# VectorE instead of GpSimd subtracts the row maximum from the first chunk of every attention block

## What is computed

```python
def _gat_layer(x, W, adj):
    proj = x @ W
    Wh, Ws = jnp.split(proj, 2, axis=-1)
    scores = Wh @ Ws.T
    a = jax.nn.softmax(scores, axis=-1) * adj
    out = a @ Wh
    out = out + x
    return jax.nn.leaky_relu(out, NEG_SLOPE)
```

## Time and profile before

| | |
|---|---|
| median of 3 runs | 1641.16 us (1640.25 to 1642.18) |
| the profiled execution, its own time | 1643.23 us |
| its span, first to last instruction | 1641.4 us |
| attention, first scores to end | about 518 to 1641 us of the span |
| PE busy | 1568.4 us, 96% of the span |
| DVE busy | 1183.7 us, 72% |
| ACT busy | 1086.6 us, 66% |
| POOL busy | 996.9 us, 61% |
| mean granted TensorE clock | 0.995 of full speed |

### The profile page before, as it was taken

One profiled execution on the slowest core, in us unless ns is written; L12 is line 12 of the kernel. 1 busy time (PEld: TensorE's weight loads), 2 busy tenths in 40 slices (PEclk: granted clock), 3 DMA queues, 4 the chain that ended last, 5 costly groups with the idle time before them and its releaser, 6 DMA issues.

```text
span 1641.4 us, 34734 instructions
## 1 busy us (share of the span) xinstructions
PE 1568.4 (96%) x12902; PEld 1542.8 (94%) x12902; DVE 1183.7 (72%) x2138; ACT 1086.6 (66%) x2115; POOL 996.9 (61%) x874
## 2 busy tenths in 40 slices
PE   5899999999999999999999999999999999999984
PEld 5899999999999999999999999999999999999984
DVE  6556767666675677777777778757777777777774
ACT  4679898988984566666666666646666666666653
POOL 1112222222220588888888888838888888888886
PEclk9999999999999999999999999999999999999999
DMA  4124444554430133333333335512333333333332
GB/s 144 39 50 118 118 123 116 126 138 116 119 95 26 53 97 97 98 97 97 97 95 96 96 97 180 166 40 84 98 101 99 97 101 100 97 98 97 98 103 71
DMA packets 88665, 163.35 MB, mean 100 GB/s; under 512 B 9265, under 2 KB 19376, under 8 KB 88240
## 3 DMA queue, kind: packets, MB, share of 16 engines
q1 hardware_dynamic: 60624, 113.41, 23.1%
q0 software_dynamic: 24336, 44.31, 11.0%
q10 hardware_dynamic: 3536, 3.41, 0.6%
HBM read 147.99 MB, written 13.11 MB: 98 GB/s over the span
## 4 chain that ended last, share of the span: by engine, by line
PE 74%; POOL 11%; issue 8%; DVE 4%; ACT 3%; DMA 0%; POOLq 0%; DVEq 0%; SPq 0%; ACTq 0%
PE PS L1116 25%; PE PS L1314 7%; PE PS L1317 7%; PE PS L1316 7%; POOL FR L427 5%; PE PS L1189 5%; PE PS L1186 5%; PE PS L1188 5%; PE PS L1187 5%; PE PS L1185 5%; POOL X L420 5%; DVE AF L941 1%; ACT FR L600 1%; ACT ROW L620 1%; POOL PAB L420 0%
## 5 line engine op out<-in xcount | busy, mean ns | idle before, releaser
L427 POOL TENSOR_TENSOR FR<-AF,FR 128x512 fp32r<-128x512 f32 x338 | 449.8, 1331 | 162.7 <-ACT FR L600 162.7
L1116 PE MATMUL PS<-FR,RB 128*128 128x256 f32 x4056 | 539.9, 282 | 4.1 <-ACT X L582 1.8
L1116 PEld LDWEIGHTS PS<-FR,RB 128*128 128x128 f32 x4056 | 500.6, 188 | 12.6 <-ACT X L582 10.9
L420 POOL TENSOR_TENSOR X<-X,ROW 128x512 f32<-128x512 f32 x294 | 397.1, 1351 | 63.1 <-ACT ROW L610 63.1
L1314 PE MATMUL PS<-FR,RA 128*128 128x256 f32 x1352 | 388.9, 288 | 26.2 <-POOL FR L427 26.1
L1317 PE MATMUL PS<-FR,RA 128*128 128x256 f32 x1352 | 379.6, 281 | 0.0
L1316 PE MATMUL PS<-FR,RA 128*128 128x256 f32 x1352 | 378.9, 280 | 0.0
L1314 PEld LDWEIGHTS PS<-FR,RA 128*128 128x128 f32 x1352 | 254.4, 188 | 37.9 <-POOL FR L427 35.5
L941 DVE TENSOR_TENSOR AF<-PS,AJ 128x512 f32<-128x512 f32 x338 | 231.2, 684 | 79.7 <-ACT PS L594 78.4
L393 POOL DMA_DIRECT2D STGT<-adjt x169 | 90.3, 535 | 296.0 <-PE PS L1189 296.0
L582 ACT ACTIVATE X<-PS 128x512 f32<-128x512 f32 x271 | 161.2, 595 | 159.0 <-DVE AF L916 154.4
(11 more groups left out here) (138 smaller groups left out, 2376.8 us busy)
## 6 DMA issues: line engine op xcount, KB each, us to landing
AJ<-adjt SPq DMA_DIRECT2D x338, 256.0 KB, 2.7
STGT<-adjt POOLq DMA_DIRECT2D x169, 256.0 KB, 3.0
xt_scratch<-ROW SPq DMA_DIRECT2D x12, 512.0 KB, 2.7
RB<-xt_scratch SPq DMA_DIRECT2D x12, 512.0 KB, 4.7
x_scratch<-X ACTq DMA_DIRECT2D x13, 256.0 KB, 2.2
ROW<-x_scratch SPq DMA_DIRECT2D x13, 256.0 KB, 3.1
out<-ROW SPq DMA_DIRECT2D x12, 256.0 KB, 3.3
X<-xt SPq DMA_DIRECT2D x1, 1536.0 KB, 11.4
```

Of the source, the lines that this page charges most:

```text
L420: nc.gpsimd.tensor_tensor(slot, slot, MB.unsqueeze(1).broadcast_to([P, 2, 256]), ALU.subtract)\
L427: nc.gpsimd.tensor_tensor(LO[g % 2], WA[g % 2], HI[g % 3].bitcast(F32), ALU.subtract)\
L1116: last = nc.tensor.matmul(out, stationary(a, k), moving(b, k), start=(k == 0 and i == 0), stop=(k == K - 1 and i == 2))
```

## The change

VectorE subtracts the row maximum from the first chunk of every block (26 of 338 chunks), in a new function `subtract_first` placed first in step E+2 of its program. GpSimd keeps the other 312 and waits for `mb_d` at the second chunk of a block. The signals are split: `sub0_d` counts the first chunks, `sub_d` the others.

```diff
+        sub0_d = sem("sub0_d")
...
             def subtract(g):
-                if g % UNITS == 0:
+
+                if g % UNITS == 1:
                     pool.wait_ge(mb_d, g // UNITS + 1)
...
-                if y is not None:
+                if y is not None and y % UNITS:
                     subtract(y)
...
             def exponent(g):
-                act.wait_ge(sub_d, g + 1)
+                if g % UNITS:
+                    act.wait_ge(sub_d, g - g // UNITS)
+                else:
+                    act.wait_ge(sub0_d, g // UNITS + 1)
...
             def keep_max(b):
                 act.wait_ge(t2_mm, b + 1)
                 if b:
-                    act.wait_ge(sub_d, UNITS * b)
+                    act.wait_ge(sub_d, (UNITS - 1) * b)
+                    act.wait_ge(sub0_d, b)
...
+            def subtract_first(b):
+                g = UNITS * b
+                dve.wait_ge(mb_d, b + 1)
+                dve.wait_ge(ev_d, g + 1)
+                slot = RING[g % SLOTS].rearrange("p (j i) -> p j i", j=2)
+                nc.vector.tensor_tensor(slot, slot, MB.unsqueeze(1).broadcast_to([P, 2, 256]), ALU.subtract)\
+                  .then_inc(sub0_d, 1)
...
             for v in range(STEPS):
                 x, e = A_AT.get(v + 1), S_AT.get(v - 1)
+                if S_END.get(v - 2) is not None:
+                    subtract_first(S_END[v - 2])
                 if e is not None:
                     maximum(e)
```

## The result

The changed kernel is slower, by about as much as forecast: 1655.76 us (median of 4 runs, 1655.07 to 1656.42) against 1640.86 us for the kernel before in the same comparison (4 runs). The ratio is 1.0085, with a 95% interval from 1.0073 to 1.0097. Forecast were 1656.3 us, against 1641.16. The profiled execution after took 1655.07 us, its span is 1653.3 us (1641.4 before).

The account below looks back on a forecast made before the run. TensorE, busy for 96% of the span, was taken as the bound, its waits at the transition between blocks deciding. 23 transitions by 0.64 us (14.7) plus 0.4 for blocks 0, 13, 25 gave +15.1 us: 1656.3 us, range 1647 to 1662.

Parts of the forecast that it names:

- The mask: VectorE's mask of the old block's last chunk, behind keep_max: 1.67 instead of 0.91 us, so +0.76.
- regular seams: The 23 like transitions between blocks (1 to 12, 14 to 24), forecast at 0.64 us each, 14.7 us in all.
- turn_sum_back: TensorE's step behind row_sum, reciprocal and spread_rec: 6.26 instead of 5.62 us after keep_max, so +0.64.
- The two side chains: Behind keep_max: new block's first eviction ends 2.37, in time for scores; GpSimd's low ends 4.58, TensorE waiting about 0.4 us.
- The 0.16 us of slack: Time left between the first chunk's delayed eviction, ending at 2.37, and TensorE's scores needing it at 2.53 after keep_max.
- GpSimd's relief at 0: GpSimd loses 26 subtracts of 1.29 us; the time was to turn into waiting, costed at 0.
- the 64.9 us in the earlier trace: GpSimd's waits for keep_max before a block's first subtract, over 26 times; the change was to take them off it.
- Nothing is caught up behind the seam: Behind the transition between blocks, the whole pipeline moves by the same 0.64 us and waits keep their length.
- The 0.81 us: TensorE's wait 14 us behind the transition between blocks, at 930.92 us, forecast to stay as long as before.
- blocks 0, 13 and 25: Blocks with transitions of their own form; at most one slot of 0.60 us each, all three put at 0.4 us together.
- held up by GpSimd: Rival: VectorE's subtract takes 1.48 instead of 0.69 us, delay 1.43 us per transition between blocks, 33 us, 1674; chance 0.08.

Follow-up runs that it names:

- e3: Changed kernel with a second VectorE instruction of the same size, changing no value, in front of the subtract: 1673.58 us, ratio 1.0189.
- e4: Changed kernel with the first chunk's subtract left out on both engines, its exponent taken with scale 0: 1641.02 us, ratio 0.9996.
- e7: e1 with VectorE's second residual (L981) moved ahead of the total: 1629.83 us, ratio 0.9925.
- e1: Changed kernel with VectorE's copy (the new block's first maximum) placed before the wait for keep_max and the subtract: 1641.66 us, ratio 0.9996.
- e2: Kernel before with only a VectorE wait for keep_max added ahead of the copy, GpSimd doing all subtracts: 1641.92 us, ratio 0.9999.
- e5: Changed kernel with the subtract moved behind the old block's last mask, before the total: 1668.07 us, ratio 1.0154.
- e8: e7 with ScalarE's exponent of the old block's last chunk ahead of keep_max and the subtract behind the mask: 1634.28 us, ratio 0.9951.
- e6: Kernel before with VectorE's second residual (L981) moved ahead of the total, GpSimd doing all subtracts: 1628.47 us, ratio 0.9917.

## Why the prediction was right

**The mask, forecast +0.76.** It is +0.72 (1.63 against 0.91). The subtract started at 0.42, not at GpSimd's 0.46. Its length is 0.69 as taken from L981, with nothing held up at the regular seams.

**turn_sum_back, forecast +0.64.** It is +0.58 at this seam (6.20 against 5.62), and 0.52 us per block by the table. The term that was mis-sized is this one, 0.64 us for each of 23 seams: the mask came 0.04 us less late than assumed, and from turn_sum_back to `keep_rec` it is 0.47 us after and 0.52 before (6.20 to 6.67 against 5.62 to 6.14), so that `keep_rec` is only 0.53 us late. By the table that is 0.12 us too much at 23 seams, 2.8 us in all.

**The two side chains.** The eviction ran at 1.75 to 2.35 (forecast 1.78 to 2.37) and TensorE's scores at 2.53 didn't wait for it. `low` ended at 4.52 (forecast 4.58) and TensorE waited 0.35 us (forecast 0.4). In e3, where the eviction ends later by a slot, TensorE does wait for it, and `turn_sum` starts late. The 0.16 us of slack were real, and small.

**GpSimd's relief at 0.** Shown by e4, and by e7 for a kernel with the next wait shortened too. The engine is off the path where it is relieved. One reading on the way was wrong: of the 64.9 us in the earlier trace rows, which the prediction says the change takes off GpSimd, 54.2 stay. They are two waits, one at the start of each layer, and now stand before the second chunk (the L422 row of the page after). At the other 24 blocks the wait was 0.45 us each. Since the relief was put at nothing, this changed no number.

**Nothing is caught up behind the seam.** The 0.81 us are 0.81 us again.

**Which part costs.** The prediction put the delay down to one slot for the subtract and one for the copy, less 0.45 us of idle time. e1 and e2 take one slot away each and both come out at the time of the kernel before; e3 adds one and costs 0.74 us a seam. That is shown.

**Where I was wrong: blocks 0, 13 and 25, put at 0.4 us together.** Block 0 is +0.09 and block 13 alone is +1.05. I had said that GpSimd has nothing to do at that moment. At blocks 0 and 13 there is no old chunk, so its first own instruction is the subtract of the second chunk, which waits for the same `keep_max`. GpSimd, VectorE and TensorE's weight loads in the timelines of the kernel after, at block 13:

```profile
1112.47 1.29 POOL L422 TENSOR_TENSOR X<-X,ROW 128x512 f32<-128x512 f32 x1 [21.47 <-ACT ROW L616]
```

```profile
1112.76 1.55 DVE L946 TENSOR_TENSOR X<-X,ROW 128x512 f32<-128x512 f32 x1
```

```profile
1115.59 1.49 PEld L1132 LDWEIGHTS PS<-FR,RB 128*128 128x128 f32 x12 [1.48 <-ACT X L584]
```

VectorE was held by the weights' low part (L904) until 1112.76, GpSimd had started 0.29 us before, and the subtract took 1.55 us instead of 0.69. That is the rival "held up by GpSimd" at 2 of 26 seams. The section "SBUF: two separate sides" of "SBUF — State Buffer" in the Trainium skill has it: the one that starts first keeps the other out for its whole instruction. The rows agree: 1112.47 + 1.29 = 1113.76, and the subtract ends 0.55 us after that, at 1114.31. Block 0 has the same 1.55 us and pays only 0.09: the eviction behind the copy starts 2.93 us after `keep_max` at both instead of 1.46, but at block 0 TensorE has 24 weight loads of other work for that time, and at block 13 it has 12 and then stands for 1.48 us.

**The tail, +1.13 us.** Of it 0.12 us are the late mask of block 25. In the tail the granted clock was lower than in the execution before: 0.94 and 0.80 of full speed on the mean of its two halves against 1.00 and 0.86. Between 1605.5 and 1607.5 us it was 0.50, so 1.2 instead of 2.4 GHz, where the kernel before kept 1.00. e1 tells the two apart, because block 25 has no copy and its tail runs the same instructions in the same order as the changed kernel's: with 1.00 and 0.85 it took 52.74 us, 0.09 more than before. So about 1 us goes with the lower clock and not with the subtract. e7's execution had the lower clock too (0.93 and 0.81), those of e3, e5 and e8 kept 1.00 in the first half. What makes it fall in one execution and not in another is open.

The two misses nearly cancel, and that is luck: 2.8 us too much at the regular seams, and 1.9 us too little at the others, of which 1 us is the clock.

## What to carry to other kernels

Before moving an instruction to an engine that is busy for only 72% of the time, look at what stands right behind the wait that it brings along, and count slots: here one fitted, and of the second 0.52 of 0.61 us were passed on at every regular seam. Put the new wait behind whatever doesn't need it; one line further down made the difference of 14 us. And an engine that waits for its input gains nothing from being relieved: look at what ended its idle time before counting its busy time.

## What the runs showed of the hardware

The largest gain of these runs came from something that no busy share shows. A VectorE instruction with both inputs in SBUF and a GpSimd instruction keep each other out, and which of them pays depends on some 0.1 us in their starts: fold_sum (256 elements) takes 0.42 us when it starts 0.11 us ahead of `low`, 1.08 us when it starts 0.49 us behind it (e5), and 1.23 us at 0.34 us behind it (e8). The mask, which has one input in PSUM, isn't held: the one at 920.02 in the kernel before runs beside GpSimd's `low` (919.19 to 920.66) and takes 0.68 us. The instruction that I had expected to be safe by being early (e8) lost 4.5 us by it, and swapping two instructions of VectorE gained 14 us (e6), as much as the change had cost.
